# A norm–attention–norm–feed-forward layer on one core: three feed-forward weight blocks before the second half's norm, and weight remainders ahead of a block's product

## The reference, cut to what matters

```python
h = layernorm(x) * (1 + ca) + sa
x = x + ga * attn(h, Wq, Wk, Wv, Wo, Wg, ...)        # gated linear attention, 32 heads
h = layernorm(x) * (1 + cb) + sb
gate = silu(einsum('bsh,ih->bsi', h, w_gate))         # 1376 rows of weights
up   = einsum('bsh,ih->bsi', h, w_up)
x = x + gb * einsum('bsi,hi->bsh', gate * up, w_down)
```

## Time and profile before

| | us |
|---|---|
| median of 3 runs (lowest, highest) | 1062.1 (1061.17, 1062.36) |
| the profiled execution's own time | 1062.45 |
| its span, first to last instruction | 1060.5 |
| PE busy in the span | 1027.9 (97%) |
| DVE busy | 759.2 (72%) |
| ACT busy | 705.5 (67%) |
| POOL busy | 215.2 (20%) |
| share of PE in the chain that ended last | 92% |

### The profile page before, as it was taken

One profiled execution on the slowest core, in us unless ns is written; L12 is line 12 of the kernel. 1 busy time (PEld: TensorE's weight loads), 2 busy tenths in 40 slices (PEclk: granted clock), 3 DMA queues, 4 the chain that ended last, 5 costly groups with the idle time before them and its releaser, 6 DMA issues.

```text
span 1060.5 us, 14275 instructions
## 1 busy us (share of the span) xinstructions
PE 1027.9 (97%) x4678; PEld 805.9 (76%) x4678; DVE 759.2 (72%) x1352; ACT 705.5 (67%) x1374; POOL 215.2 (20%) x132
## 2 busy tenths in 40 slices
PE   5889999999999999999999999999999898999998
PEld 3667777787777777777777787777777567888786
DVE  5767887887788778878887887788777975334322
ACT  3457877877788788878877877788777645233300
POOL 2212221211222221112221211222223520000000
PEclk9999999999999999999999999999999999999999
DMA  8442411220131013101401220131022303111011
GB/s 313 139 145 62 132 26 40 79 79 20 40 119 40 20 40 119 40 22 62 131 22 40 79 79 20 40 119 40 20 100 60 100 21 129 60 40 60 20 40 40
DMA packets 37947, 74.09 MB, mean 70 GB/s; under 512 B 3264, under 2 KB 19936, under 8 KB 35616
## 3 DMA queue, kind: packets, MB, share of 16 engines
q1 hardware_dynamic: 37056, 73.30, 21.5%
q10 hardware_dynamic: 864, 0.43, 0.1%
HBM read 69.38 MB, written 2.24 MB: 68 GB/s over the span
## 4 chain that ended last, share of the span: by engine, by line
PE 92%; DVE 3%; ACT 2%; issue 1%; DMA 1%; POOL 0%; SPq 0%; DVEq 0%; ACTq 0%; POOLq 0%
PE ps_q_gt L69 15%; PE ps_q_gt L71 15%; PE ps_q_gt L70 15%; PE ps_ss_o L69 6%; PE ps_ss_o L71 6%; PE ps_ss_o L70 6%; PE ps_s_y L799 5%; PE ps_kv_x L71 3%; PE ps_kv_x L70 3%; PE ps_kv_x L69 3%; PE ps_s_y L808 2%; PE ps_kv_x L822 2%; PE ps_s_y L69 2%; PE ps_s_y L71 2%; PE ps_s_y L70 2%; PE ps_ss_o L830 1%
## 5 line engine op out<-in xcount | busy, mean ns | idle before, releaser
L1867 POOL TENSOR_TENSOR q_sin<-q_sin,cst 128x512 f32<-128x512 f32 x64 | 89.4, 1397 | 300.8 <-ACT q_sin L1002 300.8
L69 PE MATMUL ps_q_gt<-hT_hi,wq_hi 128*128 128x512 f32 x256 | 125.2, 489 | 1.2 <-DVE q_cos L1388 1.2
L1855 POOL TENSOR_TENSOR dec<-dec,future 128x1024 f32<-128x1024 f32 x31 | 74.3, 2397 | 248.1 <-ACT expg L1021 248.1
L1583 DVE TENSOR_TENSOR prob<-ps_s_y,dec 128x512 f32<-128x512 f32 x63 | 43.5, 691 | 85.2 <-PE ps_s_y L799 84.5
L69 PE MATMUL ps_ss_o<-wo_hi,z_hi 128*128 128x512 f32 x260 | 102.5, 394 | 1.6 <-DVE z_lo L64 1.6
L69 PE MATMUL ps_q_gt<-hT_hi,wg_hi 128*128 128x512 f32 x256 | 103.3, 404 | 0.0
L71 PE MATMUL ps_ss_o<-wo_hi,z_lo 128*128 128x512 f32 x260 | 101.6, 391 | 0.0
L70 PE MATMUL ps_ss_o<-wo_lo,z_hi 128*128 128x512 f32 x260 | 101.5, 390 | 0.0
L71 PE MATMUL ps_q_gt<-hT_hi,wq_lo 128*128 128x512 f32 x256 | 100.7, 393 | 0.0
L71 PE MATMUL ps_q_gt<-hT_hi,wg_lo 128*128 128x512 f32 x256 | 100.6, 393 | 0.0
L70 PE MATMUL ps_q_gt<-hT_lo,wg_hi 128*128 128x512 f32 x256 | 100.5, 393 | 0.0
(11 more groups left out here) (274 smaller groups left out, 2617.2 us busy)
## 6 DMA issues: line engine op xcount, KB each, us to landing
dec<-gT_dram SPq DMA_DIRECT2D x32, 512.0 KB, 5.7
raw_q<-wq_in SPq DMA_DIRECT2D x32, 256.0 KB, 2.7
raw_g<-wg_in SPq DMA_DIRECT2D x32, 256.0 KB, 2.9
raw_o<-wo_in SPq DMA_DIRECT2D x8, 1024.0 KB, 7.1
raw_pair<-wkv_in SPq DMA_DIRECT2D x8, 512.0 KB, 4.6
raw_pair<-wgu_in SPq DMA_DIRECT2D x7, 512.0 KB, 3.3
raw_gu<-wgu_in SPq DMA_DIRECT2D x6, 512.0 KB, 3.3
x<-x_in SPq DMA_DIRECT2D x2, 1024.0 KB, 10.2
```

The costliest lines, as they stand in the source:

```text
L69: pe.matmul(out, w_hi, x_hi, start=first, stop=False)
L1583: nc.vector.tensor_tensor(prob[:], ps_s.rearrange("p (h i) -> p h i", h=GRP), dec[:, tile // 2 % 2, :, tile % 2], ALU.mult).then_inc(prob_ ...
L1855: nc.gpsimd.tensor_tensor(cells, cells, future[:].unsqueeze(1).broadcast_to([P, GRP * CPB, CHUNK]), ALU.add).then_inc(mask_done, 1)
L1867: nc.gpsimd.tensor_tensor(q2, q2, sinT, ALU.mult).then_inc(qsin_done, 1)
```

## The change

1. `FIRST_W` goes from 2 to 3. Block 2 now meets only the first half at first (step 2); place 3 comes in step 3 (first half) and step 4 (second half). There are still 22 steps, and blocks 0, 1 and 2 come again as places 11, 12 and 13 (steps 19, 20, 21): 14 places in place of 13.
2. Step 2 takes silu in one instruction, as the later steps do; the order of the norm's sets 2 to 4 and of steps 1 and 2 is written anew on PE, ACT and DVE.
3. In the loop, `split_w_hi(i + 1)` stands ahead of `ffn_silu(e)` and `split_w_lo(i + 1)` ahead of `ffn_prod(e)`. The split of place 4, which the old loop left out at step 3 (`e > EARLY_E`), and that of place 3 move with it.

```diff
-FIRST_W = 2
+FIRST_W = 3
@@ PE
             ln_turn(2)
+            ffn_gate(2)
             ln_turn(3)
-            ffn_gate(2)
+            ffn_up(2)
             ln_turn(4)
-            ffn_up(2)
@@ ACT
             ln_rstd(3)
+            ln_rstd(4)
             ffn_hi(1)
+            split_w_hi(3)
+            ffn_silu(2)
             ln_modulate(2)
-            ln_rstd(4)
             ln_modulate(3)
-            ffn_exp(2)
+            ffn_hi(2)
             ln_modulate(4)
-            split_w_hi(3)
-            ffn_sigmoid(2)
-            ffn_hi(2)
             for e in range(EARLY_E, len(FFN)):
                 i, it, half = FFN[e]
+                if e == LAST_OF[i - 1] + 1 and i + 1 < len(W_ORDER):
+                    split_w_hi(i + 1)
                 ffn_silu(e)
-                if e > EARLY_E and e == LAST_OF[i - 1] + 1 and i + 1 < len(W_ORDER):
-                    split_w_hi(i + 1)
                 ffn_hi(e)
@@ DVE
+            ln_stats(7)
+            ln_variance(4)
             ffn_prod(1)
             ln_normalise(3)
-            ln_stats(7)
-            ln_variance(4)
             ffn_lo(1)
+            split_w_lo(3)
+            ln_normalise(4)
             ln_hi(2)
-            ln_normalise(4)
+            ffn_prod(2)
             ln_lo(2)
             ln_hi(3)
             ln_lo(3)
-            ffn_cap(2)
+            ffn_lo(2)
             ln_hi(4)
             ln_lo(4)
-            ffn_gated(2)
-            split_w_lo(3)
-            ffn_prod(2)
-            ffn_lo(2)
             for e in range(EARLY_E, len(FFN)):
                 i, it, half = FFN[e]
+                if e == LAST_OF[i - 1] + 1 and i + 1 < len(W_ORDER):
+                    split_w_lo(i + 1)
                 ffn_prod(e)
-                if e > EARLY_E and e == LAST_OF[i - 1] + 1 and i + 1 < len(W_ORDER):
-                    split_w_lo(i + 1)
                 ffn_lo(e)
```

## The result

The changed kernel takes 1052.99 us (median of 4 runs, 1052.17 to 1054.42), beside 1061.82 (4 runs, 1061.17 to 1062.36) for the kernel before: ratio 0.9919, 95% interval 0.9901 to 0.9936. Two later comparisons gave 0.9925 (0.9912 to 0.9939) and 0.9924 (0.9910 to 0.9939). It is faster by some 8 to 9 us; the forecast was 8.2, and 1053.9 us. A gain in us that stands beside a ratio is worked out from the ratio; the difference of two medians can be some tenths of a us away from it.

A forecast was written before the change was run, and what follows sets the result against it. PE, busy 97% of the span, was taken as the bound, so its waits and slow matmuls could be won: 2.8 + 1.6 + 2.2 + 1.7 - 0.1 = 8.2 us, giving 1053.9 us; range 1053.0 to 1056.8.

The forecast's parts named there:

- First place: PE's wait at step 3's gate product behind step 2's `ffn_gated`: 2.8 us of waits and 1.6 of clock go, 4.4 together.
- the wait for set 3's tile: PE's old 0.43 us wait at 878.16 for set 3's normalised tile, 0.35 of it counted as won.
- The margins: Time to spare at step 4's gate: 0.9 us for the norm's second half, 0.6 for silu 3 on ACT.
- The norm's case: Rival, chance 0.10: step 4's gate waits about 1 us and the clock drops (1.6); 5.6 us won, 1056.5.
- Second place: Last gate product waits for place 12's remainder on DVE: 2.19 us of wait and 1.70 of clock go, 3.9 together.
- The table rule: Rival, chance 0.12: ACT's table load also costs a 1.38 us drain, so step 4 waits 0.5 us; 1054.4 us.
- The slower case: Rival, chance 0.02: place 5's load, queued behind `grow` and seven down blocks, lands late and ACT and PE wait.
- the clock's: Rival, chance 0.03: clock low for some 12 us more at another place, costing 6 us; 1060, no change.
- the clock's part: Slow matmuls behind the waits at step 3's gate and the last gate: 1.6 and 1.7 us, expected to go.

The follow-up runs named there:

- the two kernels with more work on ACT: Changed kernel with the norm's set 2 written twice or three times on ACT: 1053.73 us (ratio 0.9915) and 1056.84 us (0.9941).
- the loop's order alone: Kernel before with only the loop's weight splits moved ahead of silu and product, FIRST_W = 2, old norm order: 1057.73 us, ratio 0.9962.
- the old loop: Changed kernel with the weights split behind silu and product again, three blocks ahead kept: 1060.18 us, ratio 0.9985.
- the pieces: Changed kernel with step 2's silu again as exponential, cap, logarithm, exponential and multiply: 1056.45 us, ratio 0.9952.

## Why the prediction was right, point by point

**First place.** Predicted 2.8 for the waits and 1.6 for the clock, 4.4 in all. Step 4 starts at 888.53 after; before it would be 891.48 and one product of 2.72 further, 894.20. Less the 0.91 by which the stretch starts earlier, that is 4.8. The mis-sized term is the wait for set 3's tile, put at 0.35. PE now goes on with gate 2 0.79 us after the first transpose of set 2 (876.58 - 875.79), where before the next thing stood 1.46 us behind it (878.16 - 876.70): 0.67 us. I had let gate 2 start 1.05 us behind, but the tail of the transposes overlaps the product. The rest came as laid out: silu 2 at 879.68 is 3.9 us behind the transposes' start (laid out 4.15), place 3's remainder at 879.63, 3.3 early. The table load and its silu ran end to end; the last matmul of gate 2 was over at 879.56, so the load, which ended at 879.66, and not PE was what silu 2 waited for.

**The margins.** 0.9 us for the norm and 0.6 for silu 3 were forecast; the trace has 1.04 and 0.80, and the two kernels with more work on ACT a slack of 0.7. The norm's case, at 0.10, was not far off: 2 us more on ACT bring it about. Its price was too high: it took in the clock's fall, and none of the traces in which step 4 waited (0.98 us, 2.18 us, and 1.23 us behind an earlier 1.44) shows one.

**Second place.** Predicted 2.2 and 1.7, less 0.1: the stretches give 8.50 - 4.8 = 3.7, and the wait left at step 20 is 0.07 us. Place 13's remainder ends at 979.41, 3.8 us into step 20 (laid out 3.9), and place 12's at 975.54, just as PE is ready. The kernel with the loop's order alone confirms the wait part on its own.

**The table rule.** The Trainium skill ("ScalarE: Activation LUTs", What ACT_TABLE_LOAD costs) gives 1.38 us of drain beside the load's 1.28. The trace agrees on the load and not on the drain: the load starts 0.02 us behind the rounding ahead of it (877.32 + 1.04, then 878.38), and silu 2 starts 0.02 us behind the load's end. It is the same in the other traces of the changed kernel (880.41 + 1.28, then 881.71, in the second). The case of 1054.4 built on the drain is out, though one later median, 1054.40, happens to have that number.

**The slower case and the clock's.** Place 5's load was issued at 879.65 and ACT used it, without waiting, at 895.50. The mean granted clock over the span was 1.000, against 0.995 before, so no more than half a microsecond was lost elsewhere. The second trace of the changed kernel has 0.995, and there the clock was low only before 60 us and in the last microseconds, where the change does nothing.

**What was less sure than it looked: the clock.** Of the 8.2 us, 3.3 were the clock's part, taken from one trace in which it fell at both places. Counting all traces, a wait of 2.0 to 2.3 us in the steps was followed by a fall in 3 of 6 cases (before both; the old loop's first, not its second; neither in the loop's order alone nor in the pieces), the one of 4.54 us was, and those of 1.44 us and less were not. Ahead of the steps, a wait of 1.8 us that all twelve traces have at 820 to 825 us was followed by a fall in one of them, that of the loop's order alone (0.57 from 824 to 828 us), whose wait of 2.0 us at 842 was not. The waits alone are 3.0 + 2.2 - 0.1 = 5.1 us (3.0 is the stretch of the loop's order alone over the changed kernel, where the clock did not fall). The three comparisons give 8.6, 8.0 and 8.1 us, so about 3 of the 3.4 us are paid on the median of before. The clocks of the other executions speak for the same. The span times what its mean clock lacks of 1.000 is what the clock cost: 1060.5 x 0.005 = 5.3 us in the trace of before, where the three windows with 0.91 make 3 x 1.8 = 5.4. Over the 51 later executions of the kernel before this is 5.4 us in the mean, over the 15 of the changed kernel 2.6: 2.8 us of clock, give or take 1.2. The spans without it, 1054.6 and 1049.0 us in the mean, are 5.5 us apart, give or take 0.9, which fits the 5.1 of the waits. So most of the 3.4 us is paid in a usual execution of before; that it is only half (1.7) is barely within the uncertainty. Why 3 of the 6 traced waits had no fall stays open. The forecast had no case for it, and should have had one reaching to 1062.1 - 5.1 = 1057; that the clock's part came in nearly in full was in part luck.

**The median of 1052.99** lies 0.9 under the forecast, on the very edge of the range given, which began at 1053.0. The stretch explains 0.3 of that (8.50 against 8.2); the rest is in the spread of the start, as the later medians, 1054.40 and 1053.25, show.

## What to carry to other kernels

A wait that repeats wherever two instructions stand in one order is best looked for in the order: ask of each remainder which instruction it stands behind, and for what that one waits. A block of work moved ahead is cover for what comes late, but it may bring one more place where the old order waits; here the third block alone brought a fifth of the gain, the loop's order alone half. A term that comes from a low clock in one trace should be given a chance and not its full size, and the mean clocks of the other executions, where they are at hand, say how often it is paid.

## What the runs showed of the hardware

- The same wait of TensorE does not always bring the same clock: behind 2.03 us of idle time in one execution, the granted clock was 0.50 for three microseconds the first time and stayed at 1.00 the second (the old loop, three ahead). A fall costs 1.7 us in the trace of before (4.42 for a product of twelve matmuls instead of 2.72).
- An activation table load of 1.28 us began 0.02 us behind the instruction ahead of it and was followed by its first user within 0.02 us.
- Eight transposes of 128 x 128 in float32 take 1.03 us by their row, and the next product starts 0.79 us after the first of them.
